# Node-row transfers of 125 partitions issued as two: partitions 0 to 111 and 112 to 124

## The reference, cut to what matters

```
x = x + gnn_attention(layernorm(x), src, dst, relation)      # Q, K, V; softmax over the edges of each node
x = x + ffn_top_half(layernorm(x))                           # only the highest-weighted nodes get the FFN
x = x + geometric_gnn(layernorm(x), edge_vector, src, dst)   # gathers node rows by edge, sums messages by dst
x = x + shared_ffn + top2_of_8_experts(layernorm(x))         # gathers node rows by expert
```

## Time and profile before

| | |
|---|---|
| median of 3 runs | 4223.03 us (4218.73 to 4236.21) |
| profiled execution: its time, its span | 4227.08 us, 4225.4 us |
| mean granted TensorE clock | 0.793 of full speed |
| TensorE, VectorE, ScalarE, GpSimd busy | 65%, 58%, 28%, 35% of the span |
| moved by DMA | 361.08 MB, 85 GB/s over the span |

### The profile page before, as it was taken

The page is one execution under the profiler, slowest core; times in us unless marked ns, Lnnn a source line. Parts: engine busy times, 40 slices in busy tenths (PEclk is TensorE's granted clock), DMA queues, the critical chain, the costliest instruction groups (busy, mean ns, idle before and its releaser), DMA issues. The chain is left out here.

```text
span 4225.4 us, 47313 instructions
## 1 busy us (share of the span) xinstructions
PE 2753.3 (65%) x12540; PEld 1883.1 (45%) x12541; DVE 2441.5 (58%) x5663; ACT 1174.1 (28%) x4280; POOL 1494.0 (35%) x1405
## 2 busy tenths in 40 slices
PE   6445555277777762330873688888888269899970
PEld 3434443144544441220663355455554257576750
DVE  8645555398888972549021699889988420122211
ACT  0000000045555561010210244444444112233320
POOL 0877777365555520000000344444443032011124
PEclk9856665578788875655996799999999579999985
DMA  2232322876666632000001333333333052211112
GB/s 90 74 87 72 77 73 69 111 218 181 175 184 183 180 87 77 21 15 0 21 0 36 108 107 107 101 105 105 105 101 91 31 115 36 61 34 33 32 37 77
DMA packets 260903, 361.08 MB, mean 85 GB/s; under 512 B 115004, under 2 KB 191275, under 8 KB 260449
## 3 DMA queue, kind: packets, MB, share of 16 engines
q0 software_dynamic: 83488, 220.74, 19.9%
q1 hardware_dynamic: 143424, 133.26, 11.3%
q10 hardware_dynamic: 33790, 4.77, 1.0%
HBM read 325.04 MB, written 32.96 MB: 85 GB/s over the span
## 5 line engine op out<-in xcount | busy, mean ns | idle before, releaser
L1375 POOL DMA_INDIRECT g_rows<-h_d,src x416 | 397.2, 955 | 1331.3 <-SPq L1322 812.8
L307 POOL DMA_INDIRECT rec_d<-o_rec_in,o_place x400 | 485.8, 1215 | 254.0 <-issue 211.1
L1047 POOL DMA_INDIRECT a_strip<-kv_d,src x416 | 425.3, 1022 | 356.4 <-DVE x L1183 155.6
L1071 ACT ACTIVATE x<-a_strip,x 128x64 f32<-128x64 f32 x1664 | 408.5, 334 | 210.0 <-PE a_psv L1116 209.1
L1116 PE MATMUL a_psv<-x 128*125 128x260 f32 x832 | 298.0, 491 | 157.9 <-DVE agg L1210 132.2
L1452 PE MATMUL g_psa<-g_msg,g_hot 128*125 128x256 f32 x832 | 250.9, 427 | 109.8 <-DVE g_msg L1544 109.8
L391 PE MATMUL o_ps_base<-o_run,o_lo_hot_t 125*125 125x25 f32 x798 | 161.0, 350 | 217.8 <-DVE o_run L512 217.8
L1440 PE MATMUL g_pso<-w_o,g_ut 128*128 128x256 f32 x832 | 284.4, 424 | 1.9 <-ACT g_lk L1390 1.9
L1712 PE MATMUL ps_h_f<-h_t,w_f 128*128 x640 | 174.1, 433 | 161.4 <-DMA b_f<-in_L_ffn_b 136.7
L1116 PEld LDWEIGHTS a_psv<-x 128*125 128x125 f32 x832 | 172.7, 231 | 219.0 <-DVE agg L1210 129.7
L1407 ACT ACTIVATE g_msg<-g_vec,g_en 128x192 f32<-128x192 f32 x416 | 155.2, 443 | 370.8 <-DVE g_vec L1528 370.8
(11 more groups left out here) (384 smaller groups left out, 5392.4 us busy)
## 6 DMA issues: line engine op xcount, KB each, us to landing
a_row<-rows_d SPq DMA_DIRECT2D x104, 256.0 KB
o_row<-dst_rows_d SPq DMA_DIRECT2D x100, 244.1 KB
o_row_lo<-lo_rows_d SPq DMA_DIRECT2D x100, 122.1 KB
e_w<-in_L_ffn_W1p SPq DMA_DIRECT2D x8, 1024.0 KB, 17.0
e_w<-in_L_ffn_W2p SPq DMA_DIRECT2D x8, 1024.0 KB, 26.3
y_d<-e_y SPq DMA_DIRECT2D x56, 128.0 KB
a_strip<-kv_d,src POOLq DMA_INDIRECT x416
g_rows<-h_d,src POOLq DMA_INDIRECT x416
```

The source lines that it names most:

```text
L307: pool.indirect_dma_start(out=m.rec_d[:, :], out_offset=bass.IndirectOffsetOnAxis(ap=place[s % RP][:, u:u + 1], axis=0), in_=rec_in[:, U * ...
L1047: pool.indirect_dma_start(out=strip[:, lane.start + u, place:place + 2, :].rearrange("p a d -> p (a d)"), out_offset=None, in_=m.kv_d[:, : ...
L1071: act.activation(msg[b][:, u, h, 0:HD], strip[:, lane.start + u, place, h * HD:(h + 1) * HD], ACT.Copy, scale=w[:, k * U + u, h:h + 1])
L1375: pool.indirect_dma_start(out=rows[r][:, u, 64:512], out_offset=None, in_=m.h_d[:, :], in_offset=bass.IndirectOffsetOnAxis(ap=m.src[:, s * ...
```

## The change

Each direct transfer of node rows is issued as two, one of partitions 0 to 111 and one of 112 to 124: x (twice), the normalised rows, K and V, the reload of V and of the normalised rows, the node table, the expert rows and the output. The waits count the added transfers. The broadcast rows of the sort, the biases and all transfers of 128 or 104 partitions stay as they are. In `move`, the order of the list decides the queue: of the node table, SP takes both parts of the 256 and ACT both parts of the 192; of the output SP takes the first part and ACT the second; of the expert rows SP takes the first part and then the router weights, ACT the second part.

```diff
+PARTS = (slice(0, 112), slice(112, P))
...
-            sp.dma_start(m.x[:, :, :], rows(a["x"])).then_inc(s_x, 16)
+            for p in PARTS:
+                sp.dma_start(m.x[p, :, :], rows(a["x"])[p, :, :]).then_inc(s_x, 16)
...
-                    sp.dma_start(rows(m.n_d), m.h[:, :, :]).then_inc(s_out, 16)
+                    for p in PARTS:
+                        sp.dma_start(rows(m.n_d)[p, :, :], m.h[p, :, :]).then_inc(s_out, 16)
...
-                    sp.dma_start(m.kv_d[j * P:(j + 1) * P, :], kv[j % RK][:, :]).then_inc(s_kvout[j % RK], 16)
+                    for p in PARTS:
+                        sp.dma_start(m.kv_d[j * P + p.start:j * P + p.stop, :], kv[j % RK][p, :]
+                                     ).then_inc(s_kvout[j % RK], 16)
...
-                    sp.dma_start(m.v[:, gs, :], v_rows[:, gs, :]).then_inc(s_back, 16)
-                    sp.dma_start(m.h[:, gs, :], rows(m.n_d)[:, gs, :]).then_inc(s_back, 16)
-                sp.dma_start(m.x[:, :, :], rows(a["x"])).then_inc(s_x, 16)
-                sp.wait_ge(s_back, 16 * 2 * NG)
+                    for p in PARTS:
+                        sp.dma_start(m.v[p, gs, :], v_rows[p, gs, :]).then_inc(s_back, 16)
+                        sp.dma_start(m.h[p, gs, :], rows(m.n_d)[p, gs, :]).then_inc(s_back, 16)
+                for p in PARTS:
+                    sp.dma_start(m.x[p, :, :], rows(a["x"])[p, :, :]).then_inc(s_x, 16)
+                sp.wait_ge(s_back, 16 * 2 * NG * len(PARTS))
...
-            move(nc, "h", [(m.h_d[:, 0:D].rearrange("(j p) d -> p j d", p=P), m.h[:, :, :]),
-                           (m.h_d[:, D:D + 192].rearrange("(j p) d -> p j d", p=P), spun[:, :, :])])
+            plain, turned = rows(m.h_d[:, 0:D]), rows(m.h_d[:, D:D + 192])
+            move(nc, "h", [io for p in PARTS for io in ((plain[p, :, :], m.h[p, :, :]),
+                                                        (turned[p, :, :], spun[p, :, :]))])
...
-                move(nc, "wr1", [(rows(m.h2_d), m.h[:, :, :]), (wr[:, :, :], half(a["L1_ffn_Wr"]))])
+                move(nc, "wr1", [(rows(m.h2_d)[p, :, :], m.h[p, :, :]) for p in PARTS]
+                     + [(wr[:, :, :], half(a["L1_ffn_Wr"]))])
...
-        move(nc, "out", [(rows(out), m.x[:, :, :])])
+        move(nc, "out", [(rows(out)[p, :, :], m.x[p, :, :]) for p in PARTS])
```

More of the change, by code:

```diff
@@ L286, in _ @@
                     sp.wait_ge(s_take, 2 * j + 1)
-                    sp.dma_start(m.kv_d[j * P:(j + 1) * P, :], kv[j % RK][:, :]).then_inc(s_kvout[j % RK], 16)
+                    for p in PARTS:
+                        sp.dma_start(m.kv_d[j * P + p.start:j * P + p.stop, :], kv[j % RK][p, :]
+                                     ).then_inc(s_kvout[j % RK], 16)
             for r in range(RK):
-                sp.wait_ge(s_kvout[r], 16 * len(range(r, NT, RK)))
-            sp.wait_ge(s_out, 16)
+                sp.wait_ge(s_kvout[r], 16 * len(PARTS) * len(range(r, NT, RK)))
+            sp.wait_ge(s_out, 16 * len(PARTS))
             sp.wait_ge(s_nt, 36)
@@ L563, in beside @@
                 if s == 0:
-                    dve.wait_ge(s_x, 16)
+                    dve.wait_ge(s_x, 16 * len(PARTS))
                 if s < NORM - 1:
@@ L589, in beside @@
                     if j >= RK:
-                        dve.wait_ge(s_kvout[j % RK], 16 * (j // RK))
+                        dve.wait_ge(s_kvout[j % RK], 16 * len(PARTS) * (j // RK))
                     dve.tensor_tensor(kv[j % RK][:, :], ps_vk[0:P, :], b_vk[:, :], ALU.add).then_inc(s_take, 1)
@@ L2272, in fetch @@
                     gs = slice(g * G, (g + 1) * G)
-                    sp.dma_start(m.v[:, gs, :], v_rows[:, gs, :]).then_inc(s_back, 16)
-                    sp.dma_start(m.h[:, gs, :], rows(m.n_d)[:, gs, :]).then_inc(s_back, 16)
-                sp.dma_start(m.x[:, :, :], rows(a["x"])).then_inc(s_x, 16)
-                sp.wait_ge(s_back, 16 * 2 * NG)
-                sp.wait_ge(s_x, 16)
+                    for p in PARTS:
[4 more added lines that the diff above has]
+                sp.wait_ge(s_back, 16 * 2 * NG * len(PARTS))
+                sp.wait_ge(s_x, 16 * len(PARTS))
             def normalise(dve, g, slot, ch):
@@ L2283, in normalise @@
                                      rd[:, gs, :, None].to_broadcast(shape), ALU.mult))
-                dve.wait_ge(s_back, 16 * 2 * NG)
+                dve.wait_ge(s_back, 16 * 2 * NG * len(PARTS))
                 ch(dve.tensor_tensor(hd(tmp[:, :, :]), hd(m.v[:, gs, :]), dz[:, gs, :, None].to_broadcast(shape),
```

## The result

The changed kernel takes 4126.7 us, the median of four runs (4121.94 to 4135.16). The kernel before took 4222.8 on the same chip. The ratio is 0.977 (0.974 to 0.980): 96 us saved, where 134 were forecast. The result is inside the forecast range. The profiled execution of the changed kernel is the slowest of its four, 4135.16 us with a span of 4133.5.

What follows compares the result with a forecast made beforehand. No engine fills the kernel; it was taken as stages with different limits, exposed transfers using 5 of 16 DMA engines. Moves 100 (101.3 less 1 for issues) plus sort 34 save 134 us: 4089 for the median, range 4065 to 4138.

Steps and rivals of the forecast that it cites:

- the moves: Output, expert rows, node table and reload: 18.4 MB exposed, 155.6 us before, 54.3 after, 101.3 saved.
- the sort: Sort stage: GpSimd bounds it, and its waits for VectorE nearly all go; 34 us saved, bounds 17 and 35.
- at 339: Rate assumed for split transfers on 16 engines, 339 GB/s, from a 128-partition load of expert weights; bounds 190 and 370.
- 16 engines bring less: Rival for all split transfers: they spread but reach only 190 GB/s; total saving 87, time 4136 us; chance 0.12.
- a share of 1 with 200 GB/s: Sign that the prediction is wrong: DMA engines fully busy yet moving only 200 GB/s, where over 300 was expected.
- its three waits: Expected signs: SP's output wait about 10 to 11 us, node table's near 18, VectorE's idle after the reload near 20.
- the edit of the K/V stores: Sort: each broadcast row ready 1.1 to 1.3 us earlier; 22 periods give 24 to 29 us, GpSimd can take 24.2.
- n_d with its lead: Sort: faster normalised-rows store gives VectorE 20.7 us, GpSimd 10.6 at once, and leaves some 10 us of GpSimd's lead.
- The edits at nothing: First load of x and reload of x: already covered by other work, so splitting them saves nothing.
- The 13 partitions go on one engine: Rival: one engine carries 20 of 25 partitions; 31 us saved, and 14 in the sort; 4178 us; chance 0.03.
- the change does not do what it says: Rival: parts follow one another on the same few engines, issues add 7 us at most; 4223 to 4230; chance 0.03.
- SP is held: Rival in the sort: twice as many transfers hold SP longer, 36 us over 24 K/V stores; 4259 us; chance 0.02.

Runs made afterwards that it cites:

- experiment 1: Small separate kernel issuing each transfer alone, with various partition counts, between memory and on-chip memory or within memory; loads of 112 partitions 239 GB/s, of 128 300 GB/s.
- experiment 10: Small separate kernel with the same memory rows on neighbouring partitions or spread over 128, each transfer alone; 64 neighbours 204 GB/s, 64 spread 309 GB/s.
- experiment 5: Small separate kernel moving all 125 partitions, cut and queued in different ways; store of 112 beside 13 took 15.2 us, store cut by tiles 12.5 us.
- 2: Kernel before, with only the 25 K/V stores of the sort split in two; 4213.57 us, a single run.
- 3: Kernel before, with only the store of the normalised rows (n_d) split in two; 4219.54 us, a single run.
- 6: Changed kernel with the node table's two stores whole again (125 partitions), everything else split; 4144.4 us, ratio to before 0.980.
- 11: Changed kernel with one more store of 125 partitions ahead of the geometric stage, into a table written again later; 4153.65 us, ratio to before 0.981.
- 4: Kernel before, with only the reload, node table, expert rows and output split, the sort as before; 4169.38 us, ratio 0.985.
- 7: Changed kernel with V and n_d reloaded over 128 partitions, and node table, expert rows and output cut by tiles over both queues; 4115.37 us, ratio to before 0.9722.
- 8: The changed kernel once more, unaltered, on the same chip as the wide-load kernels; 4125.75 us, ratio to before 0.9757.
- experiment 9: Changed kernel with only the reload of V and n_d done over 128 partitions (wide loads); 4120.78 us, ratio to before 0.9737.

## Why the prediction was right in its mechanism, and 42 us too large

The span fell by 91.9 us, and the sum said 134 (134.3 before rounding). The difference is 42.4: 28.1 in the moves, -2.8 in the sort, 10.1 in the geometric stage and 7.0 in the rest.

**The mis-sized term: "at 339".** The step "I take 339, nearest in row size and length" put 28.1 us too much into the moves (73.2 in place of 101.3). It went wrong by 10.6 in the reload, 5.6 in the node table and 6.0 each in the expert rows and the output. The transfer did go from 5 engines to 16, as the prediction read out of five tiny packets: 29 tiny packets, share 0.34 to 1. But the row was a load to 128 partitions, of whose 3.39 MB 0.32 came by an indirect transfer beside it, and two things were not as in that row.

- The placement. A load of 128 partitions has 300 GB/s, of 112 it has 239 (experiment 1), and experiment 10 shows that the places of the partitions set the rate of a transfer alone. Of 112 and 13 one behind the other, 206 GB/s come out, and this is the reload.
- The part beside it and the tail. The store of 112 alone has 283 GB/s and took 10.1 us; with the 13 beside it on the other queue it took 15.2 (experiment 5). That is most of the 6.0 us in the output, and so probably in the expert rows, which go in the same way. The tail there is not the 13: they had landed by 4126 us, and the rest of the 112 ran on to the end at a falling share (0.28 from 4129 to 4131). In the node table the two 112s ran at 322 GB/s, near the forecast, and the loss is nearly all in the tail, at 106. Which engines end late, and why, is not shown.

The rival "16 engines bring less", at 190, was too low for the moves (58.8 us saved, where 73.2 were measured), but its mechanism is what took place: the truth lay between it and the forecast. A sign of being wrong that the prediction had named came up, "a share of 1 with 200 GB/s"; and none of its three waits came out: SP's for the output was 16.7 us and not 10 to 11, SP's for the node table some 23 (it issues for 9.2 us and waits for 13.4 more) and not near 18, VectorE's idle time 30.5 and not near 20.

**The sort.** Its term, 34, measured 36.8. The wait of 25 us is gone (the longest is 8.6). But the edit of the K/V stores was put at 24 to 29 us, held to 24.2 by what GpSimd had to give, and alone it gave 15.3; n_d with its lead was put at some 21 and alone gave 12.6, since the lead was worth 5.7 us of late waits and not 10. The sum of 34 came out because it was bounded by GpSimd's idle time, 34.8, and nearly all of that went, not because the halves were priced right. That much of it was luck.

**What was not foreseen: the geometric stage, 10.1 us longer.** No instruction of it was changed. Its counts and the gathers' own time are those of before (a median gather of 946 ns in both). What differs is the clock granted to TensorE, 0.93 over the stage in place of 0.95, and TensorE's busy time, 812 in place of 802 us. It goes with the pause ahead of the stage, in which TensorE is idle at a granted clock of 0.50, which is the lower level, 1.2 GHz:

| kernel | pause, us | stage, us | granted clock | clock in its first 200 us | 100th gather, us | 200th gather, us |
|---|---|---|---|---|---|---|
| before; 2; 3 | 50 | 914.8; 913.3; 913.3 | 0.95 | 0.91 | 209.7 to 209.9 | 431.8 to 433.6 |
| 6, node table in one | 50 | 915.2 | 0.95 | 0.91 | 210.0 | 433.8 |
| 11, pause put back | 54 | 914.5 | 0.95 | 0.91 | 209.9 | 430.0 |
| changed; 4; 7; 8; 9 | 25 to 26 | 924.9; 922.9; 922.4; 924.8; 922.7 | 0.93 to 0.94 | 0.87 to 0.88 | 214.8 to 217.4 | 440.0 to 441.4 |

Ten profiles fall into two groups without overlap, and experiments 6 and 11 put the pause back by two different edits. That the shorter pause costs 7 to 12 us behind it is shown. The last three columns, counted from the first gather, say when: 5 to 8 us are lost by the 100th of 416 gathers, 6 to 11 by the 200th, and next to nothing is added after it. These are the first 200 us, before and in the changed kernel:

```profile
2343.80:2543.80 200.00, 168.31 (x627) 96.32 (x628) 169.55 (x386) 83.81 (x314) 89.87 (x95) 0.91 0.39 107
```

```profile
2262.40:2462.40 200.00, 169.50 (x611) 95.26 (x612) 164.46 (x373) 80.05 (x299) 87.85 (x92) 0.88 0.39 106
```

TensorE is as busy and gets through fewer instructions. The prediction named the clock only as open and let it widen the range downward; it belonged into the sum as a loss. Why a longer rest ahead gives a higher clock in these first 200 us is not settled by these runs.

**What stays open.** The rest gave back 8.0 us of the span, where 1 was foreseen for issues. Attention, from its first gather to its last, is 4.4 us longer (724.9 in place of 720.5; all kernels of this study lie between 720.5 and 725.8). Another 1.8 lie around it, between the last scatter and the reload's first issue, and 1.6 between the last geometric gather and the store of the expert rows; the other stages have under 1. All of it is of the size by which runs of one kernel differ.

**The edits at nothing.** The first load of x and the reload of x stayed hidden: the first scatter starts at 103.6 us against 103.7, and SP waits 12.5 us for the reload of x while VectorE's only wait for a transfer there is the 30.5 us for V and n_d. The twenty issues of that reload held SP for up to 2.90 us each, but the last was made at 1613.1, ten us before VectorE went on. "The 13 partitions go on one engine", "the change does not do what it says" and "SP is held" are excluded by the 29 tiny packets, the share of 1 and the sort's gain.

The Trainium skill's rule against two transfers to disjoint partition halves (page "DMA: Bandwidth & Descriptors", "Rules for kernel authors") doesn't hold for 125 partitions: one transfer has 5 engines there, and issued as two the kernel was 2.3% faster. Its advice to use one of 128 partitions does hold: the wide loads took the reload's wait from 30.9 to 21.0 us in experiment 9.

## What to carry to other kernels

Before a plain transfer is priced, count the tiny packets in its stretch: they tell how many DMA engines took part, and 5 of 16 at a share of 0.34 is an invitation. A price for 16 engines must come from a row with the same partitions and the same company: 128, or 64 spread over all of them, move 300 to 340 GB/s, and 112 in a row with 13 beside them 210 to 225; so load over 128 and let the surplus rows lie where nothing is read, and cut stores so that both queues end together. And where a pause ahead of a stage bound by TensorE is shortened, compare the granted clock in the stage behind it: here 25 us saved cost 10, all within its first 440 us.

## What the runs showed of the hardware that was not expected

- 120 partitions on 15 engines are slower (174 GB/s, share 1.03) than 112 on 16 (239) and than 96 (199). More partitions and nearly as many busy engines bring less.
- A DMA share of 1 says that the engines are occupied, not what they move: it stands beside 174, 204, 239 and 341 GB/s.
- 64 neighbouring partitions take 8.0 us for 1.6 MB, and 64 of every second take 5.3.
- Two stores of 112 partitions side by side on two queues move 322 GB/s, and one of 112 with one of 13 beside it 205 to 263, though a store of 112 alone has 283.
- In this case a rest of 50 us instead of 25 bought back 7 to 12 us of 915.
